# Second attention of a two-layer kernel: a PSUM bank of its own for turned tokens, and denominators by tokens

## The reference, cut to what matters

```python
q = tanh(y @ W_Q) * pi/4;  k = tanh(y @ W_K) * pi/4       # one number per token and head
cos_KV = cumsum(cos(k) * V, axis=1); sin_KV = cumsum(sin(k) * V, axis=1)
heads  = cos(q) * cos_KV + sin(q) * sin_KV
denom  = cos(q) * cumsum(cos(k)) + sin(q) * cumsum(sin(k)) + 1e-6
attn   = einsum('dhi,btih->btd', W_O, heads / denom)
```

## Time and profile before

| what | value |
|---|---|
| median of 3 runs | 2934.99 us (2928.84 to 2935.5) |
| the profiled execution, own time | 2940.87 us |
| its span, first to last instruction | 2939.2 us |
| PE busy in the span | 2483.4 us (84%) |
| DVE busy | 1803.0 us (61%) |
| ACT busy | 1351.1 us (46%) |
| POOL busy | 812.7 us (28%) |
| mean granted TensorE clock | 0.923 of full |
| second attention, chunk 0 of sequence 0 to the end | 1363.5 to about 1972 us |

### The profile page before, as it was taken

How to read it: one execution, slowest core, us unless ns; L and a number is a source line. 1 busy time by engine, 2 the same in 40 slices (tenths; PEclk the granted TensorE clock), 3 DMA queues, 4 the chain that set the end, 5 groups by cost and what they waited for, 6 DMA issues and landing times. The chain is left out here.

```text
span 2939.2 us, 54578 instructions
## 1 busy us (share of the span) xinstructions
PE 2483.4 (84%) x20412; PEld 2258.0 (77%) x20412; DVE 1803.0 (61%) x3235; ACT 1351.1 (46%) x2053; POOL 812.7 (28%) x1194
## 2 busy tenths in 40 slices
PE   4888888994269999954677778869999999999999
PEld 3666667773169999952466667759999999999999
DVE  7555555545358888857877777826645544555444
ACT  1454445441047776743344334334445545445454
POOL 6444455503600000024556665640000000000000
PEclk8899999977589999986798888989999999999999
DMA  9993000000267777765545554514322222222222
GB/s 302 329 331 101 1 2 1 1 1 30 88 188 227 243 238 231 226 196 124 138 124 138 138 133 129 145 49 144 127 91 85 83 93 87 89 87 89 87 80 87
DMA packets 194351, 373.36 MB, mean 127 GB/s; under 512 B 28708, under 2 KB 104680, under 8 KB 193128
## 3 DMA queue, kind: packets, MB, share of 16 engines
q1 hardware_dynamic: 184792, 343.31, 38.3%
q0 software_dynamic: 9360, 27.27, 2.8%
HBM read 336.95 MB, written 100.66 MB: 149 GB/s over the span
## 5 line engine op out<-in xcount | busy, mean ns | idle before, releaser
L2305 DVE TENSOR_TENSOR e_h_lo<-e_h,e_h_hi 128x512 fp32r<-128x512 f32 x320 | 221.7, 693 | 300.5 <-ACT e_h_hi L2381 300.5
L2443 PE MATMUL e_h_ps<-e_yT_hi,e_w_hi 128*128 128x256 f32 x1280 | 362.4, 283 | 3.0 <-ACT e_h L2367 2.2
L2459 PE MATMUL e_y_ps<-e_w_hi,e_h_hi 128*128 128x256 f32 x1280 | 358.8, 280 | 2.4 <-DVE e_h_lo L2305 2.2
L2443 PE MATMUL e_h_ps<-e_yT_lo,e_w_hi 128*128 128x256 f32 x1280 | 358.3, 280 | 0.0
L2443 PE MATMUL e_h_ps<-e_yT_hi,e_w_lo 128*128 128x256 f32 x1280 | 358.2, 280 | 0.0
L2459 PE MATMUL e_y_ps<-e_w_hi,e_h_lo 128*128 128x256 f32 x1280 | 355.4, 278 | 0.0
L2459 PE MATMUL e_y_ps<-e_w_lo,e_h_hi 128*128 128x256 f32 x1280 | 355.2, 278 | 0.0
L2381 ACT ACTIVATE e_h_hi<-e_h 128x512 fp32r<-128x512 f32 x320 | 202.2, 632 | 277.1 <-DVE e_h L2300 220.8
L2367 ACT ACTIVATE e_h<-e_h_ps,e_b 128x512 f32<-128x512 f32 x320 | 219.2, 685 | 174.4 <-PE e_h_ps L2443 152.3
L2300 DVE TENSOR_TENSOR e_h<-e_h,e_spread 128x512 f32<-128x512 f32 x256 | 176.8, 691 | 133.6 <-ACT e_h L2367 132.5
L468 DVE TENSOR_REDUCE a_top<-a_ring 128x2 f32<-128x1024 f32 (+3 forms) x256 | 202.7, 819 | 84.4 <-PE a_ring L676 83.4
(11 more groups left out here) (363 smaller groups left out, 6999.6 us busy)
## 6 DMA issues: line engine op xcount, KB each, us to landing
e_w<-in_w SPq DMA_DIRECT2D x78, 1024.0 KB, 5.7
e_spread<-share_store SPq DMA_DIRECT2D x512, 128.0 KB, 2.9
a_keys<-rows_store SPq DMA_DIRECT2D x128, 256.0 KB, 4.8
a_queries<-rows_store SPq DMA_DIRECT2D x86, 256.0 KB
a_running_hidden<-rows_store SPq DMA_DIRECT2D x42, 256.0 KB
e_xs<-sorted_x SPq DMA_DIRECT2D x39, 256.0 KB, 5.4
sorted_y<-e_ys POOLq DMA_DIRECT2D x39, 256.0 KB, 5.7
e_stage_buf<-in_w_all SPq DMA_DIRECT2D x10, 512.0 KB, 3.7
```

The costliest lines, as they stand in the source:

```text
L2305: dve.tensor_tensor(h_parts[q % 2][1][:, :], h[:, q % 2, :], h_parts[q % 2][0][:, :], ALU.subtract).then_inc(h_lo.sem, h_lo.tick())
L2443: last = pe.matmul(h_ps[q % 2][:, cols], l, r, start=(m == 0), stop=(m == len(ops) - 1))
L2459: last = pe.matmul(y_ps[n][:, 0:D], h_parts[q % 2][a][:, n * P:(n + 1) * P], w2[b][:, c, :], start=(q == 0 and m == 0), stop=(q == CH - 1 ...
```

## The change

It does four things. (1) A new bank `turn_ps` takes the turned tokens, both angles and the denominators; `h_ps` keeps the hidden chunks alone. To make room for it `run_ps` is given up: the sums of j=0 live in `sums`, an SBUF tile. (2) PE's order changes with that: the waits at the head of a stage and `hidden_read` go; the first angles are found ahead of `up`, the second right behind it, `turn_back(s-1, 0)` behind `up`, `turn_back(s-1, 1)` ahead of the output product. ACT takes the first tanh ahead of the gelu. (3) The denominators are formed by tokens: four products with 128 tokens of `run` stationary and `both` moving, to 128 x (4 x 48); ACT copies them into a part of `yT`, DVE inverts 128 x 192 numbers. (4) PE turns the inverses back to 48 rows of 512 (`inverse_by_head`, c=6), and DVE multiplies from there, at the end of stage 6 instead of ahead of its scan.

```diff
+        den_tokens = yT[:, 0, 0:TB * ROWS].rearrange("p (n r) -> p n r", n=TB)
+        sums = sb("sums", [P, S])
-        v_ps, run_ps, h_ps = [ps("v0_ps"), ps("v1_ps")], ps("run_ps"), ps("h_ps")
+        v_ps, turn_ps, h_ps = [ps("v0_ps"), ps("v1_ps")], ps("turn_ps"), ps("h_ps")
...
+                if at == "inverse":
+                    dve.wait_ge(den_taken.sem, den_taken.at(1, s))
+                    dve.reciprocal(den_tokens[:, :, :], den_tokens[:, :, :]).then_inc(front_step.sem)
                 if at == "queries":
-                    dve.wait_ge(den_taken.sem, den_taken.at(1, s))
-                    dve.reciprocal(den[:, :], den[:, :]).then_inc(front_step.sem)
-                    dve.wait_ge(front_step.sem, front_step.at(3, s))
-                    dve.tensor_tensor(den[:, :], trig[:, 0, :], den[:, :], ALU.mult).then_inc(rows_ready.sem, rows_ready.tick())
+                    dve.wait_ge(den_back.sem, den_back.at(1, s))
+                    dve.tensor_tensor(den[:, :], trig[:, 0, :], turn_ps[0:ROWS, :], ALU.mult).then_inc(rows_ready.sem, rows_ready.tick())
...
-                k, out = n % 2, run_ps if j == 0 else v_ps[n % 2]
+                k, out = n % 2, sums if j == 0 else v_ps[n % 2]
...
-                row = run_ps if j == 0 else v_ps[n % 2]
+                row = sums if j == 0 else v_ps[n % 2]
...
-                k, row = n % 2, run_ps if j == 0 else v_ps[n % 2]
+                k, row = n % 2, sums if j == 0 else v_ps[n % 2]
...
                 if c == 6 and live(s + 1):
-                    front(s + 1, m, "queries")
+                    front(s + 1, m, "inverse")
...
+                if c == 6 and live(s + 1):
+                    front(s + 1, m, "queries")
                 if c == 6 and live(s + 3):
                     combine(s + 3, LEFT)
...
                 if at == "denominator":
                     act.wait_ge(den_done.sem, den_done.at(1, s))
-                    act.activation(den[:, :], h_ps[0:ROWS, :], ACT.Identity, bias=floor[0:ROWS, :]).then_inc(den_taken.sem,
-                            den_taken.tick())
+                    act.activation(den_tokens[:, :, :], turn_ps[:, 0:TB * ROWS].rearrange("p (n r) -> p n r", n=TB),
+                                   ACT.Identity, bias=floor[:, :]).then_inc(den_taken.sem, den_taken.tick())
...
+                if c == 2 and live(s + 1):
+                    front(s + 1, (s + 1) % 2, "angle0")
                 if 0 <= u < CHUNKS:
                     hidden_chunk(u)
...
                 if c == 2 and live(s + 1):
-                    front(s + 1, (s + 1) % 2, "angles")
+                    front(s + 1, (s + 1) % 2, "angle1")
+                    front(s + 1, (s + 1) % 2, "trig")
...
             def denominator(s):
                 pe.wait_ge(front_step.sem, front_step.at(2, s))
-                pe.matmul(h_ps[0:ROWS, :], both[:, :], run[:, :], start=True, stop=True).then_inc(den_done.sem,
-                        den_done.tick())
+                for n in range(TB):
+                    last = pe.matmul(turn_ps[:, n * ROWS:(n + 1) * ROWS], run[:, n * P:(n + 1) * P], both[:, :], start=True,
+                                     stop=True)
+                last.then_inc(den_done.sem, den_done.tick())
+
+            def inverse_by_head(s):
+                pe.wait_ge(front_step.sem, front_step.at(3, s))
+                for n in range(TB):
+                    last = pe.transpose(turn_ps[0:ROWS, n * P:(n + 1) * P], den_tokens[:, n, :], g.ident[:, :])
+                last.then_inc(den_back.sem, den_back.tick())
```

More of the change, by code:

```diff
@@ L1720, in _ @@
             spread_of(2)
+            front(0, 0, "inverse")
             front(0, 0, "queries")
@@ L1801, in front @@
                 if at in ("turn0", "turn1"):
[L1802 to L1806, removed]
+                    channels(s, int(at[4]), turn_ps, trF, yF_full, yF_hi, front_T[m], scale1, shift1)
+                if at in ("angle0", "angle1"):
+                    q = int(at[5])
+                    act.wait_ge(angles.sem, angles.at(q + 1, s))
+                    act.activation(trig[:, q, :], turn_ps[0:ROWS, :], ACT.Tanh).then_inc(tanhs.sem, tanhs.tick())
+                if at == "trig":
                     act.wait_ge(tanhs.sem, tanhs.at(2, s))
@@ L1834, in _ @@
             high_weights(1)
-            front(0, 0, "angles")
+            front(0, 0, "angle0")
+            front(0, 0, "angle1")
+            front(0, 0, "trig")
             norm_front(1)
@@ L1892, in turn_tokens @@
                 for n in range(TB):
-                    last = pe.transpose(h_ps[:, n * P:(n + 1) * P], src[:, n, c * P:(c + 1) * P], g.ident[:, :])
+                    last = pe.transpose(turn_ps[:, n * P:(n + 1) * P], src[:, n, c * P:(c + 1) * P], g.ident[:, :])
                 return last
@@ L1922, in find_angles @@
                     pe.wait_ge(tanhs.sem, tanhs.at(2 * s + 1))
-                product(h_ps[0:ROWS, :], [([w[:, k, q, :] for w in wqk],
+                product(turn_ps[0:ROWS, :], [([w[:, k, q, :] for w in wqk],
                                            [y[:, k, :] for y in front_T[s % 2]]) for k in range(KC)]).then_inc(angles.sem,
@@ L1966, in _ @@
             value(0)
-            pe.wait_ge(den_taken.sem, den_taken.at(1, 0))
+            inverse_by_head(0)
+            pe.wait_ge(rows_ready.sem, rows_ready.at(1, 0))
             turn_front(1, 0)
@@ L1972, in _ @@
                     value(n + 1)
-                if c == 0 and live(s + 1):
-                    pe.wait_ge(yF_full.sem, yF_full.at(1, s + 1))
-                if c in (1, 2) and live(s + 1):
-                    pe.wait_ge(yF_full.sem, yF_full.at(2, s + 1))
-                if c in (3, 4, 5) and live(s + 1):
-                    pe.wait_ge(tanhs.sem, tanhs.at(2, s + 1))
-                if c == 6 and live(s + 1):
-                    pe.wait_ge(den_taken.sem, den_taken.at(1, s + 1))
                 def bring_down():
@@ L1989, in weigh_heads @@
                         weigh(n - 2)
-                def hidden_read():
-                    if 0 <= u < CHUNKS:
-                        pe.wait_ge(hid_ready.sem, hid_ready.at(u + 1))
-                if c == 1:
+                if c in (1, 4):
+                    if c == 4:
+                        bring_down()
                     weigh_heads()
-                if c == 4:
-                    bring_down()
-                    weigh_heads()
+                if c == 2 and live(s + 1):
+                    find_angles(s + 1, 0)
                 if 0 <= u < CHUNKS:
                     up(u)
-                if c not in (4, 5):
-                    bring_down()
+                if c == 3 and live(s - 1):
+                    if live(s + 1):
+                        pe.wait_ge(tanhs.sem, tanhs.at(2, s + 1))
+                    elif live(s):
+                        pe.wait_ge(rows_ready.sem, rows_ready.at(1, s))
+                    turn_back(s - 1, 0)
                 if c == 5:
@@ L2007, in _ @@
                 if c == 0 and live(s + 1):
-                    hidden_read()
+                    pe.wait_ge(yF_full.sem, yF_full.at(1, s + 1))
                     turn_front(s + 1, 1)
                 if c == 2 and live(s + 1):
-                    hidden_read()
-                    find_angles(s + 1, 0)
-                if c == 3 and live(s - 1):
-                    hidden_read()
-                    turn_back(s - 1, 0)
+                    find_angles(s + 1, 1)
                 if c == 5 and live(s + 1):
-                    hidden_read()
+                    pe.wait_ge(tanhs.sem, tanhs.at(2, s + 1))
                     denominator(s + 1)
                 if c == 7 and live(s + 2):
-                    hidden_read()
+                    pe.wait_ge(rows_ready.sem, rows_ready.at(1, s + 1))
                     turn_front(s + 2, 0)
-                if c == 5:
+                if c != 4:
                     bring_down()
+                if c == 6 and live(s + 1):
+                    inverse_by_head(s + 1)
+                if c == 3 and live(s - 1):
+                    turn_back(s - 1, 1)
                 if c not in (1, 4, 5):
                     weigh_heads()
-                if c == 2 and live(s + 1):
-                    find_angles(s + 1, 1)
-                if c == 3 and live(s - 1):
-                    turn_back(s - 1, 1)
 E1, TOPK1, F1E = 64, 8, 64
```

3 lines of the change are left out of this document (2 added, 1 removed).

## The result

The kernel after takes 2946.98 us (median of 6 runs) against 2933.8 for the kernel before (6 runs beside them): ratio 1.0045, interval 1.0034 to 1.0057, so 13.2 us slower. The forecast was 2945, from a change of +11 us. One run in this document, of the ten of e4, ran at a granted clock of 0.64 and took 3643 us; it is left out of e4's figures.

The account below looks back on a forecast made before the run. No engine is full; DVE's work plus three stalls set each sequence of the second attention. Edits gain 27 us, contention outweighs them, together +11: profiled 2940.9 to 2952, median 5.9 lower, forecast 2945, range 2905 to 2966.

Parts of the forecast that it names:

- rival A: Scan on sums doesn't hold POOL off; only the query multiply counts: 23 us gained, 2912 us, chance 0.24.
- The one witness: A gather issued inside a scan with both inputs in SBUF took 1.14 us against 0.98; taken as sign the scan counts.
- The last step of the sum: Profiled execution going from 2940.9 to 2952, the median of runs 5.9 lower, so forecast 2945.
- The edits: Gains over the second attention's sequences, its end and start, by edits alone: 27 us.
- The contention: DVE instructions with two SBUF inputs and POOL delay each other: 6.2 us lost in each of sequences 1 to 4.
- Value product: DVE's stall for chunk 4's values: four PE blocks either way, no gain, between 1.6 gained and 1.6 lost.
- Sequence 7: Last sequence, no denominators to find: five chunks at 0.9, 1 at its stall, less 1 for freer turns: +4.5 us.
- Sequence 0: First sequence: eight chunks at 0.6 to 0.7, one or two hidden by the denominator stall: +4 - 2.3 = +1.7 us.
- Sequence 1: Second sequence of the second attention: 5 us gained by the edits alone.
- B: Contention costs as forecast but PE and POOL hold it in their slack; gain and loss cancel: about 2935, chance 0.27.
- C: POOL becomes the bound, 5.6 us a chunk against DVE's 4.6; another 0.4 us on some 40 chunks: 2961, chance 0.09.
- D: Denominators' stall stays, set by the gathers; only the reciprocal is saved, 3.8 us missing in sequences 1 to 4: 2960, chance 0.07.

Follow-up runs that it names:

- e4: The kernel before with only the denominators formed by tokens, in shared bank h_ps, turned back ahead of the up product: 2927.9 us, ratio 0.9982.
- e1: The kernel after with the j=0 scan's constant SBUF input replaced by a passed-over PSUM input: 2911.49 us, ratio 0.9936 to the kernel before.
- e3: The kernel before with run_ps made an SBUF tile and nothing else changed: 2982.86 us, ratio 1.0167.
- e8: e1 with the keys' rows stored at stage 5, only the queries' rows waiting for the denominators: 2899.04 us, ratio 0.988 to the kernel before.
- e6: The kernel after with e1's one-input scan in chunks 2 and 3 of each sequence only: 2933.86 us, ratio 0.9987 to the kernel before.

## Why the prediction held, point by point

**Right, and shown.** The two inputs from SBUF take back more than the edits give: e1 and e3 show it from both sides. The scan counts, which was the doubt between the forecast and rival A. The Newton step issued at 1582.96, 0.06 us after the scan of 1582.90, ended at 1584.10, and the scan at 1584.11. This agrees with the Trainium skill, "SBUF — State Buffer", Who interferes with whom, whose rule is that the second of the two to issue waits for the first. Two things here don't fit it exactly: the step ended together with the scan and not its own 0.20 us later, and the gather told in the last section was held off although it issued first. The one witness that the prediction had was better than its 0.16 us of delay: that gather ended 0.76 us after its scan, as the held gathers in the last section do.

In sequence 3 the contention was forecast as 6.2 us. From e1 to after the sequence grows by 6.3: by 3.3 up to the values (2.8 forecast, the Newton steps), by 0.45 in chunk 5 (0.7) and by 2.85 in chunks 7, 0 and 1 (2.7). The parts of the last sum are not as forecast. Each chunk was put at 0.9, and they are 0.1, 1.9 and 0.8; the `tensor_scalar` in chunk 0, a term that the forecast didn't have, makes 1.1 of it.

In sequence 3 the forecast for the part from chunk 4 to chunk 7 came out to the tenth: 5.8 us gained (37.0 to 31.2), 3.6 by the earlier inverse (3.8 forecast; 27.33 to 23.69 from the start of chunk 4) and 1.99 by the shorter reciprocal (2.0). It was forecast for sequences 1, 2 and 4 too, and they gained 7.3, 7.0 and 7.4, so the sequence that was read was the one with the least to gain. The stall at the denominators stayed at 5.82, in the range of 4 to 6 given. The high part's wait fell to under 2 us a sequence in 1 to 6; with the scan's contention taken away (e1) it is 1.3 us in most of them, 9.9 us in the part, so that the last 6 us of its fall are cover for DVE's longer work and no gain of the edits. ACT's piece took 0.40 (0.45 forecast), the scan on `sums` 1362 (1.3 to 1.4). DVE's waits for the keys behind the first one, at the start of sequence 0, grew as forecast, from 7.7 us to 13.2, and e8 shows their mechanism. POOL's Newton steps were the one place where a chain off DVE was charged: 2.8 us forecast, 2.1 measured on the steps.

**Mis-sized, with signs that cancel.** The mechanism was right, but that 2945 is within 2 us of 2946.98 is largely luck, as these terms show.
- *The last step of the sum*: 2952 less 5.9 is 2946, and 2945 was written.
- *POOL's sum*: near 2.0 forecast, 1.66 measured. The query multiply: near 1.1, measured 0.98 to 1.02.
- *The edits*: 27 us forecast, 22 measured (e1 against before). e1 still holds the contention of the multiply and the mixes, so what the edits give alone is not measured; chunk 7 of sequences 1 to 4, told under e1, costs 1.6 us each and was charged to the scan in part (0.9 each), which adds 0.15. By sequence e1's trace gains 2.3, 0.7, 6.4, 4.6, 4.9, 2.9 and 1.8 us and loses 5.3 in sequence 7, where 2.3, 5, 3.7, 3.7, 2.5, 3.9 and 3.9 and a gain of 1 were forecast. *The contention*: 27 + 11 = 38 forecast as the difference, 35.5 measured (after against e1, the scan's alone). The net is +13.2 where +11 stood.
- *Value product, "I take no gain here, between 1.6 gained and 1.6 lost"*: 1.5 us were lost, the far end. The step that failed is counting PE's blocks and not their clock: the blocks are as many as before, but PE enters them from 4 us of idleness and the clock is at its lower level for 3 us. In e1 the stall is 5.49 in sequences 2 to 5, so there "no gain" was right without the scan's contention.
- *Sequence 7*: +4.5 forecast, +9.0 measured. "Five chunks at 0.9" was too few: from chunk 0 to the mix all eight intervals grew, by 0.3 to 1.7 us. More than half of it isn't the scan's work, since e1 still takes 65.5 us there for 60.25, with a keys' wait of 4.12 us where it was 3.00 and one of 1.35 for the output product. Where the rest of these 5.3 us comes from stays open.
- *Sequence 0*: +1.7 forecast, -1.5 measured. Its denominators gave 3.3 us (2.74 of wait and 3.35 of reciprocal became 1.47 and 1.35), where 2.3 was forecast for all edits, and 1.2 us of waits for keys and issue at chunks 1 and 2 took up part of the contention. These waits had not been counted as cover.
- *Sequence 1*: the edits were to give 5 us, and e1 gained 0.7 (71.9 to 71.2). Its value product is 7.78 us late in e1 where it was 3.58, without the scan's contention. PE waits 4.62 us for the first tanh there, behind a table load, and then runs at clock 0.50 until 1439 in e1; in the kernel before it waited 2.02 in the same place and ran at 1.00. And the output product, which ran in that idle time before, now stands behind the second angles.

**The rivals.** A's premise fell (the scan does hold POOL off), while the time it gave for a kernel without the scan's contention, 2912, is what e1 takes, 2911.5. It put 4 us on the query multiply and 27 on the edits. Only their difference is measured, to some 7 us, and by sequence the gains lie elsewhere than forecast, so that the closeness is partly luck. B fell as an account of this kernel: PE and POOL have slack on average, but DVE's own longer instructions make most of the cost (33.9 us busier than in e1), and in chunks 2 and 3, where DVE has a stall to hide them, the chain goes through POOL's sum and 13 of the 35 us arise (e6). C fell: POOL is busy 54 of the 77.7 us of sequence 3. D is right that the stall stays, but not that the 3.8 us are missing with it, since the whole chain starts earlier.

## What to carry to other kernels

Before a tile moves from PSUM to SBUF, count the SBUF inputs of each DVE instruction that reads it, constant columns among them, and look for what POOL does at that time; here it cost 35 to 49 us, more than the 22 that the bank and the tokens gave together. If the only second input is a constant, form the operation so that it isn't needed. And when an in-order engine does a late piece first (ACT's copy of the heads here), moving the pieces around it may move a stall rather than remove it: here the value product, the denominators and the query multiply all waited, in the end, for a sum of POOL. And before a term is worked out from one sequence and taken for all, look at a second one: here the one that was read had the least to gain.

## What the runs showed of the hardware

A second input that the scan's operator passes over does not count against POOL when it lies in PSUM: in e1 the scan takes 1201 ns and POOL's sum 1323 (1289 before), with the same sums.

POOL's indirect DMA instructions are held off too. In the kernel after and in e1 the gather issued just ahead of DVE's mixes (two SBUF inputs, four in a row) takes three times its length in each of sequences 1 to 4. In e1:

```profile
1608.55 0.95 POOL L1506 DMA_INDIRECT a_zn<-sorted_y,row  x1 [0.30 <-issue]
...
1609.80 2.79 POOL L1506 DMA_INDIRECT a_mixed<-sorted_y,row  x1 [0.30 <-issue]
1610.12 0.86 DVE L1598 SCALAR_TENSOR_TENSOR x<-a_zn,share,x 128x256 f32<-128x256 f32 x2
...
1610.90 0.87 DVE L1598 SCALAR_TENSOR_TENSOR x<-a_mixed,share,x 128x256 f32<-128x256 f32 x2
```

It ends at 1612.59, 0.82 us after the mixes are over (1611.77). The traces of before, after and e1 have 21 gathers of over 1.1 us in the second attention (1, 11 and 9), and each ends 0.76 to 0.86 us after a DVE instruction with two SBUF inputs: mixes, scans of `sums`, multiplies from `sums`, and the subtractions that form the low part of the weights. The first of the two to issue doesn't always win, since this gather was issued 0.32 us ahead of the mixes. Before, the gather lay elsewhere against the mixes, and the mean of its group was 966 ns; after it is 1200.

The reciprocal goes by columns: 3345 ns for 512 and 1352 for 192 are 6.23 ns a column with 156 ns on top, while 2.7 times as many partitions cost nothing; the 258 ns of 128x16 lie within 2 ns of the same line.
